# Centring level 1's output weights once on the chip, so that eight layer norms a group read their input as it is

## What is computed

```
def layer_norm(x, g, b, eps=1e-05):
    m = jnp.mean(x, -1, keepdims=True)
    v = jnp.mean(jnp.square(x - m), -1, keepdims=True)
    return (x - m) * jax.lax.rsqrt(v + eps) * g + b
...
x = _layernorm(x + _L0_ffn_ref(...), axis=-1)
# _L1_attn_ref, for each of DEPTH = 4 layers:
#   y = y + self_attention(layer_norm(y, ln1_g, ln1_b)) @ Wo + bo
#   y = y + gelu(layer_norm(y, ln2_g, ln2_b) @ W1 + b1) @ W2 + b2
x = _layernorm(x + _L1_attn_ref(x, ...), axis=-1)
x = _layernorm(x + _L1_xattn_ref(x, ctx_512, ...), axis=-1)
```

## Time and profile before

| what | value |
|---|---|
| time, median of 3 runs | 5015.24 us (5000.78 to 5019.83) |
| profiled execution, span from first to last instruction | 4969.4 us |
| PE busy | 4410.3 us, 89% of the span |
| VectorE busy | 2640.3 us, 53% |
| ScalarE busy | 2593.2 us, 52% |
| GpSimd busy | 836.2 us, 17% |
| DMA | 183.05 MB, 37 GB/s over the span |
| mean granted TensorE clock | 0.958 of full |

### The profile page before, as it was taken

The page is one execution under the profiler, slowest core; times in us unless marked ns, Lnnn a source line. Parts: engine busy times, 40 slices in busy tenths (PEclk is TensorE's granted clock), DMA queues, the critical chain, the costliest instruction groups (busy, mean ns, idle before and its releaser), DMA issues.

```text
span 4969.4 us, 84778 instructions
## 1 busy us (share of the span) xinstructions
PE 4410.3 (89%) x29077; PEld 2535.4 (51%) x29077; DVE 2640.3 (53%) x6880; ACT 2593.2 (52%) x9813; POOL 836.2 (17%) x1454
## 2 busy tenths in 40 slices
PE   7888989989999999989799888998889888898796
PEld 3544764444454454448355444454455454554493
DVE  5555225655655655645454656556664565546523
ACT  4556434454454454453555556555655566555542
POOL 0111420011011011035021021110131021210350
PEclk9999989999999999999899989999999999999897
DMA  5000540000000000007000000000000000000172
GB/s 198 11 11 11 172 128 18 12 7 28 12 7 28 12 7 18 6 22 222 22 22 10 5 5 24 14 10 1 6 23 14 9 6 10 10 1 1 46 230 76
DMA packets 107750, 183.05 MB, mean 37 GB/s; under 512 B 13344, under 2 KB 69408, under 8 KB 107200
## 3 DMA queue, kind: packets, MB, share of 16 engines
q1 hardware_dynamic: 92544, 147.48, 9.9%
q0 software_dynamic: 13632, 28.04, 1.6%
q10 hardware_dynamic: 1152, 2.10, 0.1%
HBM read 126.33 MB, written 51.23 MB: 36 GB/s over the span
## 4 chain that ended last, share of the span: by engine, by line
PE 65%; DVE 20%; ACT 7%; issue 5%; DMA 2%; POOL 1%; SPq 0%; DVEq 0%; POOLq 0%; ACTq 0%
PE bank L713 8%; PE bank L866 7%; PE bank L883 6%; DVE rowmax L1693 6%; PE bank L745 4%; PE bank L1041 3%; PE bank L733 3%; PE bank L1152 3%; PE bank L1141 3%; PE bank L1023 3%; PE bank L790 3%; DVE probsT L1759 2%; PE bank L922 2%; PE bank L852 2%; ACT work L1323 2%
## 5 line engine op out<-in xcount | busy, mean ns | idle before, releaser
L1323 ACT ACTIVATE work<-bank,rowmax 128x128 f32<-128x128 f32 (+1 forms) x3072 | 1061.1, 398 | 208.6 <-DVE rowmax L1693 208.6
L1693 DVE TENSOR_REDUCE rowmax<-bank 128x4 f32<-128x512 f32 (+2 forms) x1152 | 614.0, 578 | 433.4 <-PE bank L866 314.8
L713 PE MATMUL bank<-mask_causal,identb 128*128 128x512 bf16 x2839 | 803.1, 394 | 22.6 <-DVE qd L1628 8.7
L883 PE MATMUL bank<-ident,work 128*128 128x128 f32 (+1 forms) x4096 | 641.0, 282 | 155.6 <-DVE probsT L1759 116.7
L1323 ACT ACTIVATION_READ_ACCUMULATOR work<-bank,rowmax 128x1 f32 x3072 | 753.1, 245 | 0.0
L883 PEld LDWEIGHTS bank<-ident,work 128*128 128x128 f32 (+1 forms) x4096 | 481.8, 144 | 377.7 <-DVE probsT L1759 196.8
L1759 DVE COPY probsT<-bank 128x512 f32<-128x512 f32 (+2 forms) x832 | 482.0, 601 | 55.3 <-PE bank L883 53.9
L713 PEld LDWEIGHTS bank<-mask_causal,identb 128*128 128x128 bf16 x2839 | 273.5, 101 | 290.7 <-issue 115.5
L866 PE MATMUL bank<-km,q 32*128 32x512 f32 (+2 forms) x1792 | 403.7, 562 | 1.9 <-issue 1.9
L2206 POOL TENSOR_TENSOR qd<-work 128x256 f32<-128x256 f32 (+1 forms) x64 | 64.7, 1012 | 1902.9 <-ACT work L1321 1836.5
L1257 ACT ACTIVATE part<-bank,eps 128x512 f32<-128x512 f32 x232 | 157.7, 680 | 383.8 <-PE bank L745 383.3
(11 more groups left out here) (336 smaller groups left out, 6902.5 us busy)
## 6 DMA issues: line engine op xcount, KB each, us to landing
slot<-in_w_L_ffn SPq DMA_DIRECT2D x78, 578.0 KB
slot<-in_w_stream SPq DMA_DIRECT2D x41, 512.0 KB
expert_rows<-slot SPq DMA_DIRECT2D x36, 516.0 KB, 6.3
slot<-in_w_L_ffn SPq DMA_DIRECT2D x39, 450.0 KB
qd<-expert_rows SPq DMA_DIRECT2D x117, 129.0 KB
back<-pair_rows SPq DMA_DIRECT2D x24, 512.0 KB, 5.3
slot<-in_w_stream SPq DMA_DIRECT2D x16, 256.0 KB
pair_rows<-qd,dest POOLq DMA_INDIRECT x234
```

Of the source, the lines that this page charges most:

```text
L713: nc.tensor.matmul(b[:], identb[:], mask["causal"][:].unsqueeze(1).to_broadcast([P, 4, P]), start=True, stop=True)
L883: ins = nc.tensor.transpose(b[0:nk, j * P:(j + 1) * P], probs[t % 2][:, r, j, 0:nk], ident[:])
L1323: ins = nc.scalar.activation(out, raw, ACT.Exp, bias=top, accum_out=expsum[t % 2][:, 4 * r + j:4 * r + j + 1])
L1693: V.tensor_reduce(m[:, 4 * r:4 * r + J], banks.where(("scores", n, c, s, r))[:, 0:J * nk] .rearrange("p (j k) -> p j k", j=J), AX_X, ALU.m ...
```

## The change

The setup block centres eight more biases (`bo` and `b2` of the four layers). The weights `Wo` and `W2` of the four layers (640 columns a layer) are loaded during the first attention into the tiles `back`, centred there by DVE (`centre_outs`: sum over 128 columns, divide, subtract), and written to a DRAM tensor `w_outs`. A level-1 slot is then filled by two DMAs, one from `w_stream` and one from `w_outs`. Eight norms a group are marked `centred`. `centre_outs` is called for the layers 0 and 1 before rounds 4 and 5 of `L0_attn` of group 0, and for 2 and 3 in group 1.

```diff
             y = X if i == 0 else "y"
-            e = norm(n + "_ln1", y, e, "hn", g=n + "_ln1", centred=i == 0)
+            e = norm(n + "_ln1", y, e, "hn", g=n + "_ln1", centred=True)
             e = mha(n, "hn", e, y, "y", D=16, mask="causal", linear=True, bo=n + "_bo")
-            e = norm(n + "_ln2", "y", e, "hn", g=n + "_ln2")
+            e = norm(n + "_ln2", "y", e, "hn", g=n + "_ln2", centred=True)
...
-        e = norm("L1_attn_ln", "u", e, X)
+        e = norm("L1_attn_ln", "u", e, X, centred=True)
...
+        centred_biases += [f"L1_{i}_{b}" for i in range(DEPTH) for b in ("bo", "b2")]
...
+        outs = [t[:].rearrange("p i s d -> p (i s d)")[:, 0:OUT_COLS] for t in back]
...
+                    def centre_outs(i):
+                        w = outs[i % 2].rearrange("p (m d) -> p m d", d=P)
+                        mean = lcol[0][:, 0:OUT_COLS // P]
+                        dve.wait_ge(*have(f"outs_loaded{i % 2}", i))
+                        link(V.tensor_reduce(mean, w, AX_X, ALU.add))
+                        link(V.tensor_scalar(mean, mean, 1.0 / P, None, ALU.mult))
+                        V.tensor_tensor(w, w, mean.unsqueeze(2).to_broadcast([P, OUT_COLS // P, P]), ALU.subtract
+                                        ).then_inc(*made("outs_centred", i))
+
                     for t in range(GROUP + 2):
+                        if n in (tagged("L0_attn", 0), tagged("L0_attn", 1)) and t in (4, 5):
+                            centre_outs(2 * st["group"] + t - 4)
                         if t < GROUP:
                             row_max(t)
...
+                    if p["outs"]:
+                        own, at = p["width"] - p["outs"][0], p["outs"][1]
+                        sp.dma_start(slots[p["slot"]][:, 0:own], src[:, 0:own]
+                                     ).then_inc(*made(f"weights{p['slot']}", p["name"] + "_in", 16))
+                        sp.dma_start(slots[p["slot"]][:, own:p["width"]], io["w_outs"][:, at:at + p["outs"][0]]
+                                     ).then_inc(*made(f"weights{p['slot']}", p["name"], 16))
+                        return
...
                 for g in range(1, GROUPS):
                     load(g)
+                load_outs(0)
+                load_outs(1)
+                keep_outs(0)
+                keep_outs(1)
+                load_outs(2)
+                load_outs(3)
+                keep_outs(2)
+                keep_outs(3)
...
+                    if p["name"] == tagged("L1_0", 0):
+                        for h in range(2):
+                            sp.wait_ge(*have(f"outs_kept{h}", DEPTH - 2 + h))
```

More of the change, by code:

```diff
@@ L45 @@
 PAIRS = 2 * TOKENS
+OUT_COLS = 128 + 512
+OUTS = {}
 def small_entries():
@@ L96, in shared_pieces @@
                           (f"L1_{i}_Wo", 128)]
+        OUTS[f"L1_{i}"] = (128, i * OUT_COLS)
         out[f"L1_{i}_mlp"] = [(f"L1_{i}_W1", 512), (f"L1_{i}_W2", 512)]
+        OUTS[f"L1_{i}_mlp"] = (512, i * OUT_COLS + 128)
     for a in ("L2_a1", "L2_a2"):
@@ L115, in piece @@
         out.append(dict(name=tagged(name, g), group=g, entries=entries, column=at[name], width=columns(entries)[1],
-                        freed=freed, block=None))
+                        freed=freed, block=None, outs=OUTS.get(name)))
     def blocks_of(name, glu):
@@ L120, in blocks_of @@
         for b in range(BLOCKS):
-            out.append(dict(name=f"{name}_b{b}", group=None, entries=[], column=0, width=width, block=(name, b),
+            out.append(dict(name=f"{name}_b{b}", group=None, entries=[], column=0, width=width, block=(name, b), outs=None,
                             freed=[("rows", (name, b))]))
@@ L2025, in list_blocks @@
                     dve.wait_ge(*have("rank", (last, CHAINS - 1)))
+                    if st["shared"]:
+                        dve.wait_ge(*have("outs_kept0", DEPTH - 2))
                     link(V.tensor_tensor(count, carry[:, ALL], W("expert_base"), ALU.subtract))
@@ L2297, in load_weights, with load_outs, keep_outs @@
                         src = io["w_stream"][:, p["column"]:p["column"] + p["width"]]
+                    if p["outs"]:
[5 more added lines that the diff above has]
+                        return
                     sp.dma_start(slots[p["slot"]][:, 0:p["width"]], src
                                  ).then_inc(*made(f"weights{p['slot']}", p["name"], 16))
+                def load_outs(i):
+                    if i >= 2:
+                        sp.wait_ge(*have(f"outs_kept{i % 2}", i - 2))
+                    for p in stream:
+                        if p["name"] in (tagged(f"L1_{i}", 0), tagged(f"L1_{i}_mlp", 0)):
+                            n, at = p["outs"][0], p["outs"][1] - i * OUT_COLS
+                            end = p["column"] + p["width"]
+                            sp.dma_start(outs[i % 2][:, at:at + n], io["w_stream"][:, end - n:end]
+                                         ).then_inc(*made(f"outs_loaded{i % 2}", i if at else ("o", i), 16))
+                def keep_outs(i):
+                    sp.wait_ge(*have("outs_centred", i))
+                    sp.dma_start(io["w_outs"][:, i * OUT_COLS:(i + 1) * OUT_COLS], outs[i % 2]
+                                 ).then_inc(*made(f"outs_kept{i % 2}", i, 16))
                 def load_rows(name, k):
@@ L2536, in program @@
         io["expert_rows"] = nc.dram_tensor("expert_rows", (ROWS, ROW), F32, kind="Internal").ap()
+        io["w_outs"] = nc.dram_tensor("w_outs", (P, DEPTH * OUT_COLS), F32, kind="Internal").ap()
         io["kept"] = nc.dram_tensor("kept", (P, BATCH * P), F32, kind="Internal").ap()
```

## The result

The changed kernel takes 5035.9 us in the median of six runs (5027.7 to 5051.8), the kernel before 5013.4 in six runs beside them (5000.8 to 5020.2): the ratio is 1.0051 [1.0034, 1.0069], 22.5 us more. The profiled execution of the changed kernel took 5036.9 us with a span of 5035.2, so only 1.7 us lie outside the span. That already shows that the 45.8 us between the span of before and its median were no fixed part of every run; the part on the prediction comes back to it.

What follows compares the result with a forecast made beforehand. It took PE and the critical chain through the norms as the bound. Terms 3 - 1.5 - 8.9 + 13 + 4.2 + 7.5 + 1.7 + 0.8 = +19.8 us on 5015.2 gave 5035 us, range 5003 to 5056.

Steps and rivals of the forecast that it cites:

- 45.8 us: Runs' median above the 4969.4 us span; taken as untouched by the change, so the sum was added to 5015.2.
- The fills pay the gain back: Chain 1's four dummy matmuls move behind real PE work, 0.86 us on the path, repaying the removed `centre`; +3 us together.
- A: Place from output projection to first up-projections, where a `centre` disappears; chain 1's `variance` +0.12 us later, 16 times.
- B: Place from down-projections to q and k, where a `centre` disappears; chain 1's `variance` +0.1 us later, 12 times.
- the fills cost nothing: Rival: chain 1's `variance` is off the path, so the gain stays; 5011, 4998 or 4994 us; chance 0.15.
- The clock at A: PE idles 2.2 us before the first up-projection; lower clock follows at half of 16 places, 1.65 us each, +13 us.
- nearly every time: Rival: the clock falls after nearly all 16 gaps at A and some at B; 5058 us; chance 0.15.
- The clock holds: Rival: the gaps before the first up-projection are harmless to the clock; 5022 us; chance 0.2.
- Blocked places, -8.9: PE's waits for chain 0's `centred` bank before chain 1's fills, as in layer 3, go away; -8.9 us.
- Setup, +4.2: Eight more biases need sixteen more weight loads and copies before the setup barrier, nothing hiding them; +4.2 us.
- The stall, +7.5: VectorE waits before round 4 of the first attention for late output-weight loads, then centres them; `row_max` +7.5 us.
- The clock behind the stall, +1.7: PE idles over 5 us behind VectorE's wait, so its next matmuls run at the lower clock; +1.7 us.

Runs made afterwards that it cites:

- e1: Changed kernel with the eight norms' dummy matmuls put back where they stood before the change, in the gap; ratio to the kernel before 0.9940, -29 us.
- e2: Changed kernel without any dummy matmuls for chain 1 of the eight norms; ratio to the kernel before 0.9962, -20 us.
- e3: Changed kernel with three more dummy matmuls in the gap before the first up-projection, the four behind it kept; ratio to the kernel before 1.0016, +8 us.
- e5: Changed kernel with all its added start work, but the eight norms centre their input as before; ratio to the kernel before 1.0021, +4 us.
- e4: Changed kernel with the output-weight loads of layers 0 and 1 issued ahead of the zeroing DMAs; ratio to the kernel before 1.0040, +21 us.
- c0: Changed kernel, unaltered, measured again beside other experiments; ratio to the kernel before 1.0054, +22 us.
- c1: Changed kernel, unaltered, measured a third time in one run on another chip; ratio to the kernel before 1.0023, +11 us.

## Why the prediction was right, and where it was not

The forecast of 5035.0 met 5035.9, inside the range of 5003 to 5056. It had "within 0.5%", below 5040, as the likeliest case; the ratio of 1.0051 [1.0034, 1.0069] lies on that boundary. The mechanism was right in its main steps. That the sum met to 1 us is luck, as the last paragraph of this section shows.

- **The fills pay the gain back** (+0.12 us a place at A, +0.1 at B). Right: a layer takes 69.6 us instead of 69.4, and e1 shows what it takes with the fills moved, 67.65. The rival "the fills cost nothing" is out: it would have left e1, e2 and e3 alike.
- **The clock at A.** The gap of 2.2 us was forecast and is 2.24. Half of the places, +13 us, was the assumption; it is 11 of 16, 18 to 19 us, and 8 to 12 in the five traces of this gap with the fills. That some half was right is luck too: the share depends on when the layers come. The rival "nearly every time" had sixteen and some at B; in its trace B's gaps of 1.84 us and C's of 1.47 were followed by none, as counted. "The clock holds" is out: e3 shows that filling the gap gives 17 us back. Out too is the rule of the Trainium skill (TensorE: Matmul & The Clock Gate, HAM oscillation), which warns of longer idle gaps only: behind this one of 2.24 us the clock fell at 63 of 112 places.
- **Blocked places, -8.9.** The waits of 2.03 us are gone, and q of place C in group 0 comes 3.4 us earlier behind `variance`. At 994.30 one can see what it gave: the layer that had it took 71.6 us before, where its neighbours took 70.2, and 72.1 now, of which 1.7 is a fall of the clock. So 1.2 were won where 1.5 was said. At 1740.02 the layer took 72.2 us before and 70.4 now, 1.8 won where 3.1 was said; the slow up passes behind it are there again, since the clock fell in the changed kernel too.
- **Setup, +4.2.** The first `row_max` is 4.4 late. Right.
- **The stall, +7.5.** It is 7.7 in the changed kernel, 8.1 in e5. The copies ended later by the setup (75.8), SP's second issue came 3.2 later than said (77.0), and what it fetched landed 6.2 us after it, the longest of its line, instead of 4.9. e4 shows the cause: with the loads ahead of the zeros there is no wait. The estimate of 2.6 us for 256 KB from the Trainium skill (DMA: Bandwidth & Descriptors, Anatomy of one DMA) would have made the stall 2 us shorter. The page fits it to DMAs issued by GpSimd, and these were issued by SP. Here the 256 KB loads behind the zeros took 4.6 us in the median, in e4 3.2.
- **The clock behind the stall, +1.7.** This term was mis-sized, and it is the step of the sum that was furthest off: I took the price of one place A. Here PE works at the lower clock for 11.7 us (88.80 to 100.50), not for a few up passes, and that, with the second `centre_outs` ahead of round 5, costs 4.5 us by round 6.
- **The 45.8 us.** The step that failed in the reasoning is the reading of the 45.8 us as something that stands around the span. There are 1.7 us around it. The span of 4969 fits the sets with medians of 4957 and 4960, and by the mark of the last section too the profiled execution of before was of their kind. That the sum could be set on the median of 5015 all the same rests on the change costing about as much on either kind, which c0 (+22) and the one run of c1 (+11) leave open.

The terms don't cancel. By the traces the start is +16.6 (13.4 and 0.8 forecast), the falls at A are +18 to 19 (13), and of the -8.9 somewhat less was won, so the sum is 27 us or more where 19.8 was forecast. The time shows 22.5, with an interval from 17 to 35 us by the ratio, which holds both. The hit to 1 us is that 19.8 stands on a median of 5015.2 and 22.5 on one of 5013.4.

## What to carry to other kernels

A dummy matmul that stands ahead of a wait is free only where the engine would idle anyway; when an edit moves it behind real work, it is on the path in full, so a change that removes work must also say where its fillers now stand. A one-off load that an in-order engine waits for belongs ahead of the bulk writes in its queue. After work is taken from a stretch in which PE waits, look at the idle time that is left, and put fillers ahead of the wait, so few that they end before the next real matmul could start.

## What the runs showed of the hardware

- **How sharp the clock's dependence is.** Behind an idle time of 1.59 us at place A the lower clock came in 0 of 64 places, behind 2.24 us in 63 of 112. Behind the 1.84 us of place B and the 1.47 of place C it never came in the seven traces that have them. Before the change it came once in 16, behind the 2.03 us wait of layer 3.
- **It is no draw.** Of the 112 places with 2.24 us, the 63 falls and the 49 others part without an exception at 2.00 us behind the last time of the grid on which the granted clock changes, with the fills behind the up-projections and without them.
- **One kernel, two kinds of chip.** Before's median was 4957 and 4960 us in two sets of runs and 5013 and 5023 in two others, over 1% apart, with a mean granted clock of before of 0.961 to 0.962 on the two faster chips and 0.957 on the slower one where it was taken beside the experiments. The traces show one more difference. The costliest group of ScalarE (busy, mean ns, idle before it and its releasers), in c0 on a slower chip and c1, the same kernel, on a faster one:

```profile
L1329 ACT ACTIVATE work<-bank,rowmax 128x128 f32<-128x128 f32 (+1 forms) x3072 | 1063.5, 399 | 222.2 <-DVE rowmax L1699 209.1 <-issue 13.0
```

```profile
L1329 ACT ACTIVATE work<-bank,rowmax 128x128 f32<-128x128 f32 (+1 forms) x3072 | 1063.4, 399 | 218.0 <-DVE rowmax L1699 218.0
```

In c0 13.0 us of its idle time wait for nothing that the profile shows; in c1 none. This holds for every trace: 8.9 to 13.0 us in the five taken in the sets with 5013 and 5023, 0.0 in the eight others, the profiled execution of before among these, whose span is 4969. These 13 us are a mark of the slower kind, not its whole cost: set side by side, the 68 us between c0 and c1 build up in small steps over the whole program, and 26 of them are there at level 1's first up-projection (818.37 and 792.12). What the engines wait for there, and whether the lower clock of these executions follows from it, no run here tells.
